# A 40-column third tile in the encoder's layer normalisations, in place of an overlapping one of 128

## What is computed

```python
def _ln(x, g, b, eps=1e-05):
    m = jnp.mean(x, axis=-1, keepdims=True)
    v = jnp.mean((x - m) ** 2, axis=-1, keepdims=True)
    return (x - m) * jax.lax.rsqrt(v + eps) * g + b
...
for l in range(LAYERS):                      # 6
    ...                                      # attention: o
    x = _ln(x + o, ln1_g[l], ln1_b[l])
    ff = jax.nn.gelu(x @ W1[l].T + b1[l], approximate=False) @ W2[l].T + b2[l]
    x = _ln(x + ff, ln2_g[l], ln2_b[l])
```

## Time and profile before

| | before |
|---|---|
| median of 3 runs (lowest to highest) | 821.42 us (821.26 to 821.55) |
| span of the profiled execution, first to last instruction | 819.1 us |
| median less span | 2.3 us |
| TensorE busy, share of the span | 98% |
| VectorE, ScalarE, GpSimd busy | 77%, 56%, 31% |
| granted TensorE clock | full in all 40 slices of the span |

### The profile page before, as it was taken

The page is one execution under the profiler, slowest core; times in us unless marked ns, Lnnn a source line. Parts: engine busy times, 40 slices in busy tenths (PEclk is TensorE's granted clock), DMA queues, the critical chain, the costliest instruction groups (busy, mean ns, idle before and its releaser), DMA issues.

```text
span 819.1 us, 16629 instructions
## 1 busy us (share of the span) xinstructions
PE 801.5 (98%) x6060; PEld 751.4 (92%) x6060; DVE 633.9 (77%) x1287; ACT 460.6 (56%) x829; POOL 251.6 (31%) x297
## 2 busy tenths in 40 slices
PE   9999999999999999999999999999999999999988
PEld 8998789999999999899999989999998999999758
DVE  5786693778778876778797887878778787876796
ACT  4386424433333336585786777667687767745421
POOL 0002120410111100364366147335525623633020
PEclk9999999999999999999999999999999999999999
DMA  5010946998889812010210021031012103010001
GB/s 191 1 52 1 373 124 253 328 323 310 317 309 337 321 53 107 1 40 14 100 44 0 17 98 38 13 102 38 4 39 72 38 13 102 26 82 1 1 0 30
DMA packets 18290, 88.36 MB, mean 108 GB/s; under 512 B 3120, under 2 KB 7472, under 8 KB 12240
## 3 DMA queue, kind: packets, MB, share of 16 engines
q1 hardware_dynamic: 18256, 87.90, 30.4%
HBM read 85.05 MB, written 2.84 MB: 107 GB/s over the span
## 4 chain that ended last, share of the span: by engine, by line
PE 47%; issue 23%; POOL 18%; DVE 8%; ACT 3%; DMA 1%; POOLq 0%; SPq 0%; DVEq 0%; ACTq 0%
PE bank L1139 14%; POOL W_L L2000 7%; PE bank L1176 6%; POOL HF_L L2058 4%; POOL arena L1981 3%; POOL WQKV_L L2000 3%; PE bank L746 2%; PE bank L872 2%; PE bank L1185 2%; PE bank L722 2%; PE bank L1049 2%; PE bank L788 1%; POOL SQ L2019 1%; PE bank L1123 1%; PE bank L1490 1%
## 5 line engine op out<-in xcount | busy, mean ns | idle before, releaser
L1139 PE MATMUL bank<-arena 128*128 (+1 forms) x1024 | 117.8, 274 | 0.0
L1139 PEld LDWEIGHTS bank<-arena 128*128 128x128 f32 x1024 | 117.4, 192 | 0.0
L1981 POOL TENSOR_TENSOR arena<-arena,srec 111x456 f32<-111x456 f32 x56 | 52.3, 962 | 125.1 <-DVE srec L2153 125.1
L2000 POOL TENSOR_TENSOR W_L<-LW,W_H 128x256 fp32r<-128x256 f32 x96 | 68.5, 752 | 36.9 <-DVE XHL L2589 33.5
L2058 POOL TENSOR_TENSOR HF_L<-arena,HF_H 128x296 fp32r<-128x296 f32 x48 | 43.8, 937 | 76.7 <-ACT HF_H L1896 76.7
L788 PE MATMUL bank<-XHL,W_H 128*128 128x296 f32 x288 | 65.1, 307 | 0.0
L1896 ACT ACTIVATE arena<-bank,vec 128x296 f32<-128x296 f32 x96 | 48.8, 509 | 20.4 <-PE bank L788 15.4
L2012 POOL TENSOR_TENSOR QW<-QW,arena x14 | 22.4, 1600 | 119.0 <-DVE QW L2490 65.6
L1330 PE MATMUL bank<-HF_L,W_H 128*128 128x296 f32 x192 | 57.4, 299 | 0.0
L1330 PE MATMUL bank<-HF_H,W_H 128*128 128x296 f32 x192 | 57.4, 299 | 0.0
L1330 PE MATMUL bank<-HF_H,W_L 128*128 128x296 f32 x192 | 57.3, 299 | 0.0
(11 more groups left out here) (276 smaller groups left out, 2205.4 us busy)
## 6 DMA issues: line engine op xcount, KB each, us to landing
arena<-ew_in SPq DMA_DIRECT2D x16, 2048.0 KB, 9.0
arena<-ew_in SPq DMA_DIRECT2D x16, 1024.0 KB, 7.0
LW<-lw_in SPq DMA_DIRECT2D x12, 1024.0 KB, 5.0
arena<-route SPq DMA_DIRECT2D x32, 185.0 KB, 3.2
LW<-lw_in SPq DMA_DIRECT2D x6, 768.0 KB, 4.3
fp_weights<-arena SPq DMA_DIRECT2D x1, 2048.0 KB, 6.4
arena<-fp_weights SPq DMA_DIRECT2D x1, 2048.0 KB, 7.2
arena<-patches_in SPq DMA_DIRECT2D x2, 864.0 KB, 7.4
```

What stands on the lines that cost most here:

```text
L1139: last = mm(o[:, m * CAP:(m + 1) * CAP], w[:, kc, mi * P:(mi + 1) * P], xg(kc, e), start=(kc == 0), stop=(kc == C - 1))
L1981: nc.gpsimd.tensor_tensor(v, v, srec[0:QROWS, s:s + 2, :].unsqueeze(3).to_broadcast([QROWS, 2, C * JH, KEYS]), ALU.mult).then_inc(p_ready, 1)
L2000: last = nc.gpsimd.tensor_tensor(low[:, cols], value[:, cols], high[:, cols], ALU.subtract)
```

## The change

For the encoder's normalisations (those whose `seq` is a tuple) the third tile starts at column 256 and holds the 40 columns that are left. Its two variance matmuls load 40 columns and write 40 partitions; its spread transpose reads 40 partitions of the reciprocals, with an identity of 40 by 40, and writes 40 columns. The partitions 40 to 127 of the third variance column keep what stood there before; root and reciprocal run over them still, and nothing reads the results. Line numbers below these functions grow by 3 and 6.

```diff
@@ ln_var_of
-                for t, (t0, _) in enumerate(var_tiles(nt)):
+                tiles = [(t0, P) for t0, _ in var_tiles(nt)]
+                if isinstance(seq, tuple):
+                    tiles[2] = (2 * P, nt - 2 * P)
+                for t, (t0, rows) in enumerate(tiles):
                     for c in range(nch):
                         at = VAR_AT + t * VAR_W
-                        last = mm(ln_bank(seq, h)[:, at:at + VAR_W], sq[:, h, c, t0:t0 + P], ones[:, 0:VAR_W],
+                        last = mm(ln_bank(seq, h)[0:rows, at:at + VAR_W], sq[:, h, c, t0:t0 + rows], ones[:, 0:VAR_W],
                                   start=(c == 0), stop=(c == nch - 1))
@@ ln_bcast_of
-                for t, (t0, _) in enumerate(var_tiles(nt)):
-                    last = nc.tensor.transpose(ln_bank(seq, h)[:, t0:t0 + P], ln_rs[:, h, t:t + 1].to_broadcast([P, P]),
-                                               ident)
+                tiles = [(t0, P) for t0, _ in var_tiles(nt)]
+                if isinstance(seq, tuple):
+                    tiles[2] = (2 * P, nt - 2 * P)
+                for t, (t0, rows) in enumerate(tiles):
+                    last = nc.tensor.transpose(ln_bank(seq, h)[:, t0:t0 + rows],
+                                               ln_rs[0:rows, h, t:t + 1].to_broadcast([rows, P]), ident[0:rows, 0:rows])
```

## The result

The changed kernel takes 826.64 us (median of 4 runs, 826.53 to 827.39), the kernel before, beside it on the same chip, 821.34 us (4 runs, 821.01 to 821.55). The ratio is 1.0066 with a 95% interval of 1.0052 to 1.008: slower by 5.3 us. The profiled execution spans 824.8 us against 819.1, at a granted clock of 1.00 in both.

A forecast was written before the change was run, and what follows sets the result against it. TensorE bounds the encoder loop, busy 69.88 of 71 us. Terms 1.8 + 2.1 - 0.9 + 0.9 + 0.95 + 0.7 = 5.6 us on a median of 821.42 gave 827.0 us, 0.7% slower; range 822.0 to 829.0.

The forecast's parts named there:

- likeliest case: Loads of 40 columns (variance) and 40 rows (spread) both stop TensorE on entry and exit: 827.0 us, chance 0.60.
- three parts: Added time from first variance to second (1.8 + 2.1 - 0.9), behind the second (0.9 + 0.95), and last half-layer (0.7 us).
- the time outside the span: Median time beyond the profiled execution's 819.1 us span: 2.3 us, taken as untouched by the change.
- The variance's hold: TensorE's stops entering and leaving the two 40-column variance passes: +0.165 us each, 1.8 us over eleven first normalisations.
- the rival that only rows hold: The 40-row spread load is stopped, the 40-column variance load gains 0.10 us: 822.7 us, chance 0.23.
- The spread's hold, first normalisation: TensorE's stops around the 40-row spread transpose before the scores: +0.19 us each, 2.1 us over eleven half-layers.
- What the scores give back: At six half-layers whose score waits for VectorE, about 0.15 us of the delay is absorbed each: -0.9 us.
- The second spread's hold: Stops around the second normalisation's 40-row transpose: 0.19 us at five half-layers without a waiting mean, 0.95 us; upper bound 0.25.
- The second variance covered by the reciprocal: VectorE's reciprocal wait, about 0.3 us, hides the variance delay, except six waiting means at 0.15 us each: 0.9 us.
- The last half-layer: The half-layer without attention has no cover, so two variance and two spread delays count fully: 2 x 0.165 + 2 x 0.19 = 0.7 us.
- the short tile is simply shorter: Neither short load is stopped; first normalisations gain 0.10 + 0.05 us each: 819.2 us, faster, chance 0.07.
- the holds vanish in waits: Encoder waits of some 10 us absorb nine tenths of the 5.6 us of stops: 822.0 us, same, chance 0.10.

## Why the prediction was right, and where it was not

The prediction (827.0 us, slower by 0.7%) came out at 826.64. Its likeliest case, that both short tiles are held, is the one that the chip shows. That the number is so close is in part luck. Its three parts were 3.0, 1.85 and 0.7 us and measure 2.9, 2.2 and 0.6 in the profiled executions, so the errors mostly cancel; and it took the time outside the span as 2.3 us, where every execution with both on record has 1.8 (1.75 to 1.91). By that the profiled execution of the kernel before was a fast one of about 820.9 us, which is why the spans differ by 5.7 us and the medians by 5.3. Term by term:

**The variance's hold**: 0.165 us by the prediction, 0.157 measured. It was read off transposes of 64 rows for matmuls of 40 columns, on the ground that both name a part of the array. The kernels with 64 and 65 columns show that ground right, and the rival that only rows hold, at 822.7, wrong.

**The spread's hold, first normalisation**: 0.19 predicted. The three steps are now 203, 176 and 239 ns where they were 109, 115 and 210: 0.185.

**What the scores give back**: 0.9 us in all, and in all that is right, but it lies otherwise. Two holds are 0.34 us; a stretch with a waiting score grew by 0.23, one without by 0.30. So 0.11 comes back at each of six and 0.04 at each of five, some 0.9 together, where the prediction had 0.15 at six alone. The stretch from the first variance to the second sums to 6 x 0.23 + 5 x 0.30 = 2.9 against the 3.0 predicted (1.8 + 2.1 - 0.9).

**The second spread's hold** was mis-sized: 0.19 taken, and 0.25 as its upper bound; its steps are 203, 176 and 354 ns where they were 109, 109 and 252, which is 0.263. The last of the three is the step behind the projection's first matmul, a long one of 296 columns, and it slows by 0.10 where the scores' slowed by 0.03. The prediction named this possibility, and set its bound too low.

**The second variance covered by the reciprocal** is the step that failed. Its first half was right: the spread's start didn't move, and its wait fell from 3.7 us for eleven to 2.0 for ten. But the prediction let the late bank on VectorE count only where a mean waits. The kernel with the 40 columns there alone shows it count everywhere, 0.13 to 0.15 us. In the whole change this error stays small, because two paths lead out of the second normalisation and the later one decides. Where no mean waits, the spread's own hold of 0.26 exceeds VectorE's 0.15, and the stretch grew by 0.267, as much as with the spread's hold alone. Where one waits, the hold disappears in it and VectorE's 0.15 decides, and it grew by 0.148. Predicted were 0.19 and 0.15, that is 1.85 us in all; measured 5 x 0.267 + 6 x 0.148 = 2.2.

**The last half-layer**: 0.7 predicted, "no such cover". Its phase has no attention; its first variance starts at 738.60 us before and 743.75 after. From there to the first matmul of L1330 (749.58 before, L1336 at 754.89 after) the changed kernel loses only 0.16 us, so here a cover was overlooked. In the kernel before, the first up-projection (L803, 741.93) starts 0.33 us after the matmul ahead of it; now that distance is 0.13. The views name no releaser for its load, but it comes 0.65 us after ScalarE's copy starts in both kernels (741.25 and 741.90, 746.56 and 747.22). So in all likelihood the chain over VectorE and ScalarE sets it. That chain starts at the spread's last transpose, and TensorE's slower steps behind that transpose fall into the gap.

Its second normalisation lies behind that matmul, 760.65 us before and 765.96 after. TensorE at its variance, its spread and the final normalisation's variance, before and then after:

```profile
760.65 0.88 PE L746 MATMUL bank<-ones_d,SQ 128*128 128x64 f32 x6
...
762.60 0.49 PE L755 MATMUL bank<-const,ln_rs 128*128 128x128 f32 x3
...
768.05 1.55 PE L746 MATMUL bank<-ones_d,SQ 128*128 128x64 f32 x12 [0.41 <-ACT SQ L1534]
```
```profile
765.96 0.89 PE L749 MATMUL bank<-ones_d,SQ 128*128 128x64 f32 x6
...
768.08 0.56 PE L761 MATMUL bank<-const,ln_rs 128*128 128x128 f32 x3
...
773.78 1.55 PE L749 MATMUL bank<-ones_d,SQ 128*128 128x64 f32 x12 [0.41 <-ACT SQ L1540]
```

Here nothing covers either hold: from variance to spread 2.11 us and not 1.96, from spread to the final variance 5.71 and not 5.45, together 0.42 us. The other kernels agree: from the matmul of L1330 to the end of the span, the kernel with the short variance alone takes 0.17 us more than the kernel before, the one with the short spread alone 0.27, the changed kernel 0.43. The last half-layer so costs 0.16 + 0.42 = 0.6 us.

**The rivals.** That the short tile is simply shorter stood at 819.2 us. The tile of 65 columns, which names the whole array, does just that and takes 818.98. The rule of the Trainium skill cited for it, "TensorE: Matmul & The Clock Gate", Part 3, The mechanism, lets a load overlap running matmuls where its row group doesn't conflict with theirs. The trace shows no such overlap for the loads of 40 rows, 0.17 us of idle time before each of 23. These loads name 64 of the very 128 rows that the running matmuls name, so by the rule's own condition it need not give them an overlap: it doesn't support this rival, and the trace doesn't contradict it. That the holds vanish in waits stood at 822.0, by waits of "some 10 us"; the lines of the earlier trace rows sum to 13.7. But those for GpSimd, over half of it, took up nothing (4.0 and 3.3 us before, 4.0 and 3.4 after), and those for the reciprocal and for the mean only a part.

## What to carry to other kernels

When a tile is made shorter, look at which part of the array its instruction names before counting the columns it saves: in the variance a lone tile of 40 or 64 columns among full ones cost 0.16 or 0.18 us, and one of 65 saved 0.1. Where a remainder is small, split the whole evenly (99, 99, 98 in place of 128, 128, 40), and where a short tile can't be avoided, put it first behind a wait, where the array is idle. A wait that covers a longer step on one engine covers nothing for a second engine which is fed by the same stream.

## What was not expected of the hardware

- A hold costs next to nothing from an idle array: 12 ns behind GpSimd's squares, 157 ns within a stream.
- Distances between variance matmuls follow the columns loaded and not the 64 that are streamed: 59 ns for 65 columns, 87 for 99, 112 for 128. A 40-column pass inside its hold takes 87, longer than one of 65 outside.
- Transposes of fewer rows gain nothing here: with 65 or 99 rows, the spread up to the scores takes the 0.33 to 0.34 us that it took with 128.
- How slowly a stream takes up its pace behind a hold differs by what follows: the step behind the first long matmul grew by 0.03 us before the scores and by 0.10 before the projection.
